# Turning two thirds of a gate and up product round: stationary weights in a routed expert kernel on one core

## The chip, the cores and the metric

The kernel runs on one core of one Trainium2 chip. The metric is the device time of one execution in microseconds. Before the change, three runs gave 753.37, 755.38 and 756.12 us; the median is 755.38.

A core has five engines with instruction streams of their own: TensorE (PE, whose weight loads are listed apart as PEld), VectorE (DVE), ScalarE (ACT), GpSimd (POOL) and SyncE (SP), which issues most transfers. They meet through semaphores. A matmul has a stationary operand, loaded by LDWEIGHTS, and a moving operand, whose columns are streamed through the array.

## The reference

One layer: layer norm, linear attention with a decaying state, a residual, a second layer norm, and a mixture of experts with one shared expert. The change touches the experts alone. With `x` of 4096 tokens by 256, 32 experts of 192 channels and 4 experts chosen for each token:

```python
g = jax.nn.silu(jnp.einsum('th,eih->tei', xf, gate_w))
u = jnp.einsum('th,eih->tei', xf, up_w)
routed = jnp.einsum('tei,ehi,te->th', g * u, down_w, combine)
sg = jax.nn.silu(xf @ shared_gate_w.T)
su = xf @ shared_up_w.T
shared = sg * su @ shared_down_w.T
return (routed + shared).reshape(b, s, h)
```

`combine` holds the softmax of the four best router scores times 1.8, and zero for the other experts. All is float32.

## The kernel before

The first part (`steps`, nine steps over eight sequences) does the attention and the router, and beside it loads, turns and splits expert weights. Each weight is kept in SBUF as two float16 halves, a high part and the rest, in one long tensor `W`: for each expert four blocks of gate and up (two halves of the 256 inputs, each high and low, each block GU = 384 columns wide: 192 gate and 192 up channels), and four blocks of down, 256 columns wide. Experts from the 24th on come from `w_late`, which the host lays out in that form (`laid_out`), and are split during the first tiles.

The second part is a loop over 191 tiles of 128 rows: 32 tiles of the shared expert, whose rows are tokens in order, then 159 routed tiles, each of one expert, whose rows were gathered into lists in DRAM. A tile goes through these stations:

- SP loads its rows (`load_tile`), already split into two float16 halves.
- PE turns them, `turn_in`, L1183: four transposes of 128x128 into PSUM. DVE copies the result to `xT` (`turn_out`, L1048) and signals `xT_done`.
- PE makes gate and up, L1212: six matmuls into `psG`, tokens stationary and the weights moving, 384 columns each (high by high, high by low, low by high, for each half of the inputs). The result has tokens on partitions and 384 channels along the free axis.
- ACT takes silu of the gate part (L664), DVE multiplies by the up part (L1072), ACT makes the high float16 half (L671, into `halves`), DVE the low one (L1091 and L1092) and signals `a_split`.
- PE turns this activation so that channels lie on partitions, L1232: three transposes of 128x128. The first 128 channels high, the remaining 64 high and low together, and the first 128 low. ACT copies them to `aT` (L668, 128x384) and signals `aT_done`.
- PE makes the down product, L1245: five matmuls of 256 columns with `aT` stationary. ACT scales it by the token's share (L680) and POOL adds it to an accumulator in DRAM by an indirect DMA (L640).

The order on each engine is written out by hand. `pe_tile(t)` issues in this order: the gate and up matmuls of tile t (behind the wait for `xT_done`), the register work of a routed tile, the turn of x for tile t+1 (L1183), the turn of the activation of tile t-1 (behind the wait for `a_split`), the down product of tile t-2 (behind `aT_done`), and more register work. The tiles overlap so that TensorE always has a stage of another tile to do.

The register work: a routed tile's weights lie at an offset in `W` that is known only at run time. `weights(t, off, width)` gives the slice, and `pe.lower_ap(...)` computes its address into registers ahead of its use, four for down at L1220 and four for gate and up of the next tile at L1249. Once in eight tiles the offsets of the next eight are fetched (`experts_of`, L1191 and L1193).

The last part of the kernel adds up three accumulators for each sequence and stores the output.

Of the kernel before, what the change touches and what calls it, by code (L numbers as in the profile page):

```python
# [5 lines left out]
def moe_block(nc, x, w_qkv, w_out, decay_param, router_w, router_b, gate_w, up_w, down_w,  # L6
# [6 lines left out]
    P = 128  # L13
# [35 lines left out]
    with ctx:  # L49
# [81 lines left out]
        half_word = carve(I)  # L131
        matched, share, token = carve(DEEP * K), carve(DEEP), carve(DEEP).bitcast(i32)
# [9 lines left out]
        halves = [words.bitcast(f16) for words in (half_word, carve(I))]  # L142
        aT = [carve(3 * P // 2).bitcast(f16).rearrange("p (n t) -> p n t", n=3) for _ in range(2)]
# [60 lines left out]
        psA = [bank[:, 0:3 * P // 2].bitcast(f16) for bank in (psV, psT[2])]  # L204
# [146 lines left out]
        def load_experts(eng, b):  # L351
# [3 lines left out]
            if b == 0:  # L355
                q0 = 1
                for src, dst in ((shared_gate_w[0:P], gu_nat[:, 0, 0]), (shared_gate_w[P:I], gu_nat[0:IC, 0, 1]),
                                 (shared_up_w[0:P - IC], gu_nat[IC:P, 0, 1]), (shared_up_w[P - IC:I], gu_nat[:, 0, 2]),
                                 (shared_down_w.rearrange("(c p) i -> p c i", p=P), dn_nat[:, 0, :, 0:I]),
                                 (shared_down_w[:, P:I].rearrange("(c p) i -> p c i", p=P), dn_nat[:, 0, :, I:I + IC])):  # L360
                    eng.dma_start(dst, src).then_inc(wstage_loaded, 16)
            e = PREP * b - 1 + q0
            which = slice(e, e + PREP - q0)
            for src, dst in ((gate_w[which, 0:P], gu_nat[:, q0:PREP, 0]), (gate_w[which, P:I], gu_nat[0:IC, q0:PREP, 1]),
                             (up_w[which, 0:P - IC], gu_nat[IC:P, q0:PREP, 1]), (up_w[which, P - IC:I], gu_nat[:, q0:PREP, 2])):
                eng.dma_start(dst, src.rearrange("e p h -> p e h")).then_inc(wstage_loaded, 16)
# [278 lines left out]
        def _(act):  # L645
# [11 lines left out]
            def act_tile(t):  # L657
# [7 lines left out]
                if a_tile(t - 1):  # L665
                    u = (t - 1) % 2
                    act.wait_ge(a_turned, t)
                    nc.scalar.activation(aT[u].rearrange("p n t -> p (n t)"), psA[u], ACT.Copy).then_inc(aT_done, 1)  # L668
                if a_tile(t):
                    act.wait_ge(a_done, t + 1)  # L670
                    nc.scalar.activation(halves[t % 2][:, 0:I], act32[t % 2], ACT.Copy).then_inc(a_hi_done, 1)  # L671
# [123 lines left out]
        def _(dve):  # L795
# [265 lines left out]
            def dve_tile(t):  # L1061
# [26 lines left out]
                if a_tile(t):  # L1088
                    dve.wait_ge(a_hi_done, t + 1)
                    both = halves[t % 2]  # L1090
# [21 lines left out]
        def _(pe):  # L1112
# [88 lines left out]
            def pe_tile(t):  # L1201
# [5 lines left out]
                if a_tile(t):  # L1207
                    pe.wait_ge(xT_done, t + 1)
                    n = 0
                    for sx, sw in ((0, 0), (0, 1), (1, 0)):  # L1210
                        for h in range(HC):
                            last = nc.tensor.matmul(psG[t % 2][:, 0:GU], xT[t % 2][:, sx, h], weights(t, (2 * h + sw) * GU, GU),  # L1212
                                                    start=(n == 0), stop=(n == 3 * HC - 1))
                            n += 1
# [13 lines left out]
                if a_tile(t - 1):  # L1228
                    u = (t - 1) % 2
                    pe.wait_ge(a_split, 2 * t)  # L1230
                    for n in range(3):
                        last = nc.tensor.transpose(psA[u][:, n * P:(n + 1) * P], halves[u][:, n * P:(n + 1) * P], ident16[:, :])  # L1232
                    last.then_inc(a_turned, 1)
# [6 lines left out]
                if a_tile(t - 2):  # L1240
                    u = t % 2
                    pe.wait_ge(aT_done, t - 1)
                    parts = ((0, 0, P), (1, 1, P), (2, 0, P), (0, 2, P), (1, 3, P))
                    for n, (part, q, height) in enumerate(parts):
                        last = nc.tensor.matmul(psY[u], aT[u][0:height, part], weights(t - 2, GUW + q * H, H, height), start=(n == 0), stop=(n == len(parts) - 1))  # L1245
                    last.then_inc(y_ready, 1)
                if routed_tile(t + 1):
                    for part in range(2 * HC):
                        pe.lower_ap(weights(t + 1, part * GU, GU))  # L1249
# [128 lines left out]
def laid_out(gate, up, down):  # L1378
# [4 lines left out]
    gu = _np.concatenate([gate, up], axis=1).reshape(n, 2 * i, h // 128, 128).transpose(0, 3, 2, 1).reshape(n, 128, -1)  # L1383
# [25 lines left out]
```

## Time and profile before

| | us |
|---|---|
| median of three runs | 755.38 |
| lowest and highest run | 753.37, 756.12 |
| span of the profiled execution, first to last instruction | 707.9 |
| between that span and the median of the runs | 47.5 |
| PE matmuls busy | 603.2 (85%) |
| DVE, ACT, POOL busy | 512.6, 434.9, 440.3 |
| mean granted clock of TensorE | 0.938 |

The profile records one execution. Its span runs from the first to the last instruction; what lies around it in a timed run isn't in it, and for the profiled execution only the span is on the page. So a change in the span is taken over to the median, with the 47.5 us left as they are. A busy time adds the stretches in which an engine has an instruction under way; matmuls are pipelined, so a record (say 220 ns for 128 columns) is longer than the distance from one to the next. That distance, not the record, is what a matmul costs in a full stream. Register work of TensorE's sequencer is not counted as busy but is listed when its line is asked for.

### The profile page before, as it was taken

What the parts mean: (1) busy time and instruction counts of PE and PEld (TensorE: products, weight loads), DVE (VectorE), ACT (ScalarE), POOL (GpSimd) and SP (SyncE); (2) the same over time, 40 slices, a digit from 0 to 9 for tenths busy, and PEclk for the clock granted to TensorE, in tenths of its full rate; (3) what the DMA queues carried; (4) which work ended last, traced back from release to release, by engine and by line L of the source; (5) the groups of instructions that cost most, each with busy time, mean ns of one, the idle gap of its engine ahead of it and who ended that gap; (6) DMA issues with size and microseconds to landing.
All of it is one profiled execution on the core that took longest, in us unless ns stands there. A gap on an engine that the chain in (4) does not pass through costs nothing.

```text
span 707.9 us, 15496 instructions
## 1 busy us (share of the span) xinstructions
PE 603.2 (85%) x4725; PEld 417.4 (59%) x4725; DVE 512.6 (72%) x1966; ACT 434.9 (61%) x1045; POOL 440.3 (62%) x367
## 2 busy tenths in 40 slices
PE   3898877897888899899999999999999999999000
PEld 2565544565555565677777777776777777776000
DVE  2588898989889968877766666666666666666164
ACT  2646445463636433688878878787788878788000
POOL 3031148658585776777078778887888888888300
PEclk9989999899999969999999999999999999999555
DMA  9664585959667676999589889888988888886799
GB/s 275 265 182 120 160 240 176 301 194 271 197 203 226 202 229 205 302 335 336 164 148 144 139 140 143 140 141 140 143 140 149 140 140 142 141 145 91 189 412 385
DMA packets 121460, 140.41 MB, mean 198 GB/s; under 512 B 22626, under 2 KB 110210, under 8 KB 120834
## 3 DMA queue, kind: packets, MB, share of 16 engines
q1 hardware_dynamic: 88816, 97.29, 44.4%
q0 software_dynamic: 29040, 38.68, 33.1%
q10 hardware_dynamic: 3522, 3.44, 1.5%
q8 instruction: 40, 0.66, 0.4%
q14 instruction: 42, 0.34, 0.2%
HBM read 79.19 MB, written 64.89 MB: 204 GB/s over the span
## 4 chain that ended last, share of the span: by engine, by line
PE 60%; DVE 19%; issue 6%; DMA 6%; POOL 4%; SPq 3%; ACT 2%; POOLq 0%; ACTq 0%; DVEq 0%
PE psD L1245 13%; PE psQ L1212 11%; PE psK L1212 11%; PE psT L1183 6%; PE psD L1296 4%; DMA acc_scratch<-arena 3%; DVE W L875 2%; DVE W L870 2%; SPq L514 2%; PE psK L1261 2%; PE psQ L1261 2%; DMA W<-acc_scratch 2%; PE psT L1232 2%; PE psV L1261 2%; PE psV L1232 2%
## 5 line engine op out<-in xcount | busy, mean ns | idle before, releaser
L640 POOL DMA_INDIRECT acc_scratch<-arena x159 | 251.3, 1581 | 73.2 <-issue 34.7
L586 POOL DMA_INDIRECT xlist_scratch<-list_row,dest x128 | 133.7, 1045 | 35.6 <-issue 34.1
L1245 PE MATMUL psD<-W,arena 128*128 (+1 forms) x955 | 135.5, 273 | 1.0 <-DVE arena L1044 0.9
L1048 DVE COPY arena<-psT 128x512 f16<-128x512 f16 x191 | 81.0, 424 | 69.2 <-PE psT L1183 68.6
L1212 PE MATMUL psK<-W,arena 128*128 (+1 forms) x576 | 109.3, 326 | 0.5 <-DVE arena L1048 0.5
L1212 PE MATMUL psQ<-W,arena 128*128 (+1 forms) x570 | 108.2, 326 | 0.1
L1245 PEld LDWEIGHTS psD<-W,arena 128*128 128x128 f16 x955 | 85.2, 98 | 8.0 <-DVE arena L1044 1.1
L671 ACT ACTIVATE arena<-arena 128x192 f16<-128x192 f32 x191 | 69.2, 362 | 13.9 <-DVE arena L1072 2.2
L680 ACT ACTIVATE arena<-psD,arena 128x256 f32<-128x256 f32 x159 | 72.8, 458 | 3.4 <-DMA acc_scratch<-arena 3.1
L1183 PE MATMUL psT<-ident,arena 128*128 128x128 f16 x764 | 74.0, 220 | 0.4 <-issue 0.4
L1183 PEld LDWEIGHTS psT<-ident,arena 128*128 128x128 f16 x764 | 57.0, 98 | 29.3 <-issue 7.2
L1091 DVE TENSOR_TENSOR arena<-arena 128x64 f16<-128x64 f32 x191 | 43.0, 225 | 40.4 <-ACT arena L671 40.4
L1212 PEld LDWEIGHTS psK<-W,arena 128*128 128x128 f16 x576 | 50.6, 97 | 33.7 <-DVE arena L1048 1.1
L1212 PEld LDWEIGHTS psQ<-W,arena 128*128 128x128 f16 x570 | 50.1, 97 | 32.4 <-DVE arena L1048 0.2
L566 POOL TENSOR_TENSOR W<-W 128x512 f32<-128x512 f32 x16 | 20.3, 1270 | 71.4 <-DVE W L870 71.3
L1092 DVE TENSOR_TENSOR arena<-arena 128x128 f16<-128x128 f32 x191 | 54.4, 285 | 0.0
L668 ACT ACTIVATE arena<-psT 128x384 f16<-128x384 f16 x95 | 46.6, 490 | 10.0 <-PE psT L1232 5.6
L668 ACT ACTIVATE arena<-psV 128x384 f16<-128x384 f16 x96 | 47.0, 490 | 7.4 <-PE psV L1232 2.1
L875 DVE SCALAR_TENSOR_TENSOR W<-psT,W 128x384 f16<-128x384 f32 (+1 forms) x72 | 40.0, 588 | 13.6 <-ACT W L720 13.6
L1296 PE MATMUL psD<-W 128*128 128x256 f32 x128 | 36.3, 447 | 11.6 <-DVE W L890 11.5
L720 ACT ACTIVATE W<-psT 128x384 f16<-128x384 f32 (+1 forms) x72 | 35.6, 528 | 16.5 <-PE psT L1139 8.5
L664 ACT ACTIVATE arena<-psK 128x192 f32<-128x192 f32 x96 | 31.7, 330 | 20.4 <-PE psK L1212 20.0
(164 smaller groups left out, 1084.8 us busy)
## 6 DMA issues: line engine op xcount, KB each, us to landing
arena<-xlist_scratch SPq DMA_DIRECT2D x159, 136.0 KB
W<-acc_scratch SPq DMA_DIRECT2D x24, 512.0 KB, 12.7
acc_scratch<-arena SPq DMA_DIRECT2D x16, 512.0 KB, 5.9
arena<-in_L_attn_x_dram SPq DMA_DIRECT2D x10, 512.0 KB, 5.1
arena<-in_L_ffn_down_w_dram SPq DMA_DIRECT2D x23, 192.0 KB, 4.9
xlist_scratch<-pad_scratch SPq DMA_DIRECT2D x32, 136.0 KB, 3.6
list_row<-xrow_scratch SPq DMA_DIRECT2D x32, 136.0 KB
acc_scratch<-arena SPq DMA_DIRECT2D x33, 128.0 KB, 12.4
```

The source lines that it names most:

```text
L586: nc.gpsimd.indirect_dma_start(xlist[:, :], bass.IndirectOffsetOnAxis(ap=dest[:, n:n + 1], axis=0), list_row[j % LISTS][:, :], None).then_ ...
L640: nc.gpsimd.indirect_dma_start(acc[t % ACCS][:, :], bass.IndirectOffsetOnAxis(ap=token[:, (t - NT) % DEEP:(t - NT) % DEEP + 1], axis=0), y ...
L668: nc.scalar.activation(aT[u].rearrange("p n t -> p (n t)"), psA[u], ACT.Copy).then_inc(aT_done, 1)
L671: nc.scalar.activation(halves[t % 2][:, 0:I], act32[t % 2], ACT.Copy).then_inc(a_hi_done, 1)
L680: nc.scalar.activation(y_sb[(t - 2) % ROUND], psY[t % 2], ACT.Copy, scale=share[:, (t - 2 - NT) % DEEP:(t - 2 - NT) % DEEP + 1]).then_inc( ...
L875: nc.vector.scalar_tensor_tensor(dst, bank_of("prep", n)[:, 0:width], WS, hi, ALU.mult, ALU.subtract).then_inc(prep_lo, 1)
L1048: nc.vector.tensor_copy(xT[t % 2].rearrange("p s c t -> p (s c t)"), psX[t % 2]).then_inc(xT_done, 1)
L1092: nc.vector.tensor_tensor(both[:, 2 * P:3 * P], act32[t % 2][:, 0:P], both[:, 0:P], ALU.subtract).then_inc(a_split, 1)
L1183: last = nc.tensor.transpose(psX[t % 2][:, n * P:(n + 1) * P], xg[t % XG][:, n * P:(n + 1) * P], ident16[:, :])
L1212: last = nc.tensor.matmul(psG[t % 2][:, 0:GU], xT[t % 2][:, sx, h], weights(t, (2 * h + sw) * GU, GU), start=(n == 0), stop=(n == 3 * HC - 1))
L1245: last = nc.tensor.matmul(psY[u], aT[u][0:height, part], weights(t - 2, GUW + q * H, H, height), start=(n == 0), stop=(n == len(parts) - 1))
L1296: last = nc.tensor.matmul(psD[:, j // 2, (j % 2) * H:(j % 2 + 1) * H], attnT[:, c, j * P:(j + 1) * P], wout_sb[:, c, :], start=(c == 0), s ...
```

## The change

Gate and up are made in three groups instead of one. The first 128 channels of gate, and the first 128 of up, are made with the weights stationary and the tokens moving, so they come out with channels on partitions, six matmuls of 128 columns for each. The remaining 64 of gate and 64 of up are made as before, together, in six matmuls of 128 columns, with tokens on partitions. For this the up weights are stored with their last 64 channels first, so that both remainders are adjacent. In `psG` each group lies where its channels lay, so that silu, product and split run unchanged.

The first 128 channels of the activation then already lie as the down product needs them, and their high and low halves are used straight from `halves`. Only the block with the 64 remaining channels (high and low) is turned and copied. `halves` gets a third buffer, since it is now read one tile later. The register work at the end of `pe_tile` prepares twelve slices instead of four: for each block two stationary operands (`for_matmul_weights=True`) and one moving one.

```diff
-        halves = [words.bitcast(f16) for words in (half_word, carve(I))]
-        aT = [carve(3 * P // 2).bitcast(f16).rearrange("p (n t) -> p n t", n=3) for _ in range(2)]
+        halves = [words.bitcast(f16) for words in (half_word, half_two, carve(I))]
+        aT = [carve(P // 2).bitcast(f16) for _ in range(2)]
...
-                    nc.scalar.activation(aT[u].rearrange("p n t -> p (n t)"), psA[u], ACT.Copy).then_inc(aT_done, 1)
+                    nc.scalar.activation(aT[u], psA[u], ACT.Copy).then_inc(aT_done, 1)
...
-                    n = 0
-                    for sx, sw in ((0, 0), (0, 1), (1, 0)):
-                        for h in range(HC):
-                            last = nc.tensor.matmul(psG[t % 2][:, 0:GU], xT[t % 2][:, sx, h], weights(t, (2 * h + sw) * GU, GU),
-                                                    start=(n == 0), stop=(n == 3 * HC - 1))
-                            n += 1
+                    products = [(sx, sw, h) for sx, sw in ((0, 0), (0, 1), (1, 0)) for h in range(HC)]
+                    whole = psG[t % 2][:, 0:GU]
+                    rest = whole.rearrange("p (m i) -> p m i", m=2)[:, :, P:I]
+                    for to, off in ((whole[:, 0:P], 0), (whole[:, I:I + P], 2 * P)):
+                        for n, (sx, sw, h) in enumerate(products):
+                            nc.tensor.matmul(to, weights(t, (2 * h + sw) * GU + off, P), xT[t % 2][:, sx, h],
+                                             start=(n == 0), stop=(n == len(products) - 1))
+                    for n, (sx, sw, h) in enumerate(products):
+                        last = nc.tensor.matmul(rest, xT[t % 2][:, sx, h], weights(t, (2 * h + sw) * GU + P, P),
+                                                start=(n == 0), stop=(n == len(products) - 1))
                     last.then_inc(gu_ready, 1)
...
                     pe.wait_ge(a_split, 2 * t)
-                    for n in range(3):
-                        last = nc.tensor.transpose(psA[u][:, n * P:(n + 1) * P], halves[u][:, n * P:(n + 1) * P], ident16[:, :])
-                    last.then_inc(a_turned, 1)
+                    nc.tensor.transpose(psA[u], halves[(t - 1) % 3][:, P:2 * P], ident16[:, :]).then_inc(a_turned, 1)
...
                     pe.wait_ge(aT_done, t - 1)
-                    parts = ((0, 0, P), (1, 1, P), (2, 0, P), (0, 2, P), (1, 3, P))
-                    for n, (part, q, height) in enumerate(parts):
-                        last = nc.tensor.matmul(psY[u], aT[u][0:height, part], weights(t - 2, GUW + q * H, H, height), start=(n == 0), stop=(n == len(parts) - 1))
+                    both = halves[(t - 2) % 3]
+                    high, rest, low = both[:, 0:P], aT[u], both[:, 2 * P:3 * P]
+                    parts = ((high, 0), (low, 0), (high, 2), (rest, 1), (rest, 3))
+                    for n, (part, q) in enumerate(parts):
+                        last = nc.tensor.matmul(psY[u], part, weights(t - 2, GUW + q * H, H), start=(n == 0), stop=(n == len(parts) - 1))
                     last.then_inc(y_ready, 1)
                 if routed_tile(t + 1):
                     for part in range(2 * HC):
-                        pe.lower_ap(weights(t + 1, part * GU, GU))
+                        for off in (0, 2 * P):
+                            pe.lower_ap(weights(t + 1, part * GU + off, P), for_matmul_weights=True)
+                        pe.lower_ap(weights(t + 1, part * GU + P, P))
...
-    gu = _np.concatenate([gate, up], axis=1).reshape(n, 2 * i, h // 128, 128).transpose(0, 3, 2, 1).reshape(n, 128, -1)
+    gu = _np.concatenate([gate, up[:, 128:], up[:, :128]], axis=1).reshape(n, 2 * i, h // 128, 128).transpose(0, 3, 2, 1).reshape(n, 128, -1)
```

Two more lines of `load_experts` load the up weights in the new order, with the same number and sizes of transfers, and `psA` shrinks like `aT`.

## Rows read from the trace of the kernel before

**Rows 1.** Part 1 of the page: busy us, share of the span, instructions.
```profile
PE 603.2 (85%) x4725; PEld 417.4 (59%) x4725; DVE 512.6 (72%) x1966; ACT 434.9 (61%) x1045; POOL 440.3 (62%) x367
```
**Rows 2.** By stretch: us; busy PE, PEld, DVE, ACT, POOL; clock; DMA share, GB/s.
```profile
280.20:345.00 64.80, 61.62 (x568) 44.49 (x569) 50.30 (x176) 51.85 (x142) 44.06 (x46) 1.00 0.90 296
345.00:655.50 310.50, 308.87 (x2879) 222.97 (x2878) 210.32 (x1118) 247.60 (x642) 245.61 (x156) 1.00 0.85 140
```
**Rows 3.** The chain that ended last, one routed tile: start us, us, what.
```profile
501.93 0.98 PE psK L1212 x6
502.91 0.22 PE psT L1183 x4
503.13 0.17 PE psT L1232 x3
503.30 0.55 PE psD L1245 x5
```
**Rows 4.** Timeline of a routed tile: start us, us, engine, line, operation, tiles, count.
```profile
352.03 1.14 PE L1212 MATMUL psQ<-W,arena 128*128 x6
...
352.77 0.28 DVE L1092 TENSOR_TENSOR arena<-arena 128x128 f16<-128x128 f32 x1
...
353.00 0.39 PE L1183 MATMUL psT<-ident,arena 128*128 128x128 f16 x4
...
353.39 0.71 PE L1245 MATMUL psD<-W,arena 128*128 x5
353.43 0.43 DVE L1048 COPY arena<-psT 128x512 f16<-128x512 f16 x1 [0.37 <-PE psT L1183]
...
353.90 0.78 PEld L1212 LDWEIGHTS psK<-W,arena 128*128 128x128 f16 x6
353.94 1.14 PE L1212 MATMUL psK<-W,arena 128*128 x6
...
354.68 0.29 DVE L1092 TENSOR_TENSOR arena<-arena 128x128 f16<-128x128 f32 x1
```
**Rows 5.** Timeline where the first tile's gate waits for the copy.
```profile
279.75 0.42 DVE L1048 COPY arena<-psT 128x512 f16<-128x512 f16 x1
...
280.22 0.50 PE L1212 MATMUL psK<-W,arena 128*128 128x384 f16 x2 [0.47 <-DVE arena L1048]
```
**Rows 6.** Line 1249 from 352 to 354: ns min/median/max, first to last start us.
```profile
L1249 PEldq FUSED_REGOPS  x2: 74/74/74, 353.1 to 353.3; - x2
```
**Rows 7.** A list-fetch tile from 353.8 to 355.5, by line; weight loads; waits, 300 to 650.
```profile
L1191 PEldq TENSOR_LOAD <-arena x1: 602/602/602, 353.9 to 353.9; - x1
...
L1193 PEldq FUSED_REGOPS  x1: 176/176/176, 354.6 to 354.6; - x1
...
L1220 PEldq FUSED_REGOPS  x2: 69/72/74, 354.8 to 354.9; - x2
...
355.06 0.23 PEld L1183 LDWEIGHTS psT<-ident,arena 128*128 128x128 f16 x4 [0.38 <-issue]
...
L1249 PEldq FUSED_REGOPS  x2: 74/76/79, 355.2 to 355.4; - x2
...
PEld psT L1183 <- issue: 7.2, 19, 0.6
```
**Rows 8.** Timeline of a router product, weight loads ahead of 32-column matmuls.
```profile
245.44 0.25 PEld L1348 LDWEIGHTS psD<-rwT,arena 128*128 128x128 f16 x6
```
**Rows 9.** Part 5 of the page: groups, busy us and mean ns of one.
```profile
L1183 PEld LDWEIGHTS psT<-ident,arena 128*128 128x128 f16 x764 | 57.0, 98 | 29.3 <-issue 7.2
...
L668 ACT ACTIVATE arena<-psT 128x384 f16<-128x384 f16 x95 | 46.6, 490 | 10.0 <-PE psT L1232 5.6
```
**Rows 10.** Line 1249 near 417.5, and the matmuls that stand ahead of it.
```profile
L1249 PEldq FUSED_REGOPS  x2: 74/74/74, 417.5 to 417.6; - x2
...
417.89 0.71 PE L1245 MATMUL psD<-W,arena 128*128 x5
```
**Rows 11.** Timeline of GpSimd in a routed tile.
```profile
500.93 1.56 POOL L640 DMA_INDIRECT acc_scratch<-arena  x1 [0.30 <-ACT arena L680]
```

More of the change, by code:

```diff
@@ L131, in moe_block @@
         half_word = carve(I)
+        half_two = carve(I)
         matched, share, token = carve(DEEP * K), carve(DEEP), carve(DEEP).bitcast(i32)
@@ L203, in moe_block @@
         psN = [psK, psQ]
-        psA = [bank[:, 0:3 * P // 2].bitcast(f16) for bank in (psV, psT[2])]
+        psA = [bank[:, 0:P // 2].bitcast(f16) for bank in (psV, psT[2])]
         psY = [psD[:, 0, 0:H], psD[:, 1, 0:H]]
@@ L357, in load_experts @@
                 for src, dst in ((shared_gate_w[0:P], gu_nat[:, 0, 0]), (shared_gate_w[P:I], gu_nat[0:IC, 0, 1]),
-                                 (shared_up_w[0:P - IC], gu_nat[IC:P, 0, 1]), (shared_up_w[P - IC:I], gu_nat[:, 0, 2]),
+                                 (shared_up_w[P:I], gu_nat[IC:P, 0, 1]), (shared_up_w[0:P], gu_nat[:, 0, 2]),
                                  (shared_down_w.rearrange("(c p) i -> p c i", p=P), dn_nat[:, 0, :, 0:I]),
@@ L364, in load_experts @@
             for src, dst in ((gate_w[which, 0:P], gu_nat[:, q0:PREP, 0]), (gate_w[which, P:I], gu_nat[0:IC, q0:PREP, 1]),
-                             (up_w[which, 0:P - IC], gu_nat[IC:P, q0:PREP, 1]), (up_w[which, P - IC:I], gu_nat[:, q0:PREP, 2])):
+                             (up_w[which, P:I], gu_nat[IC:P, q0:PREP, 1]), (up_w[which, 0:P], gu_nat[:, q0:PREP, 2])):
                 eng.dma_start(dst, src.rearrange("e p h -> p e h")).then_inc(wstage_loaded, 16)
@@ L667, in act_tile @@
                     act.wait_ge(a_turned, t)
-                    nc.scalar.activation(aT[u].rearrange("p n t -> p (n t)"), psA[u], ACT.Copy).then_inc(aT_done, 1)
+                    nc.scalar.activation(aT[u], psA[u], ACT.Copy).then_inc(aT_done, 1)
                 if a_tile(t):
                     act.wait_ge(a_done, t + 1)
-                    nc.scalar.activation(halves[t % 2][:, 0:I], act32[t % 2], ACT.Copy).then_inc(a_hi_done, 1)
+                    nc.scalar.activation(halves[t % 3][:, 0:I], act32[t % 2], ACT.Copy).then_inc(a_hi_done, 1)
                 if a_tile(t - 2):
@@ L1089, in dve_tile @@
                     dve.wait_ge(a_hi_done, t + 1)
-                    both = halves[t % 2]
+                    both = halves[t % 3]
                     nc.vector.tensor_tensor(both[:, I:2 * P], act32[t % 2][:, P:I], both[:, P:I], ALU.subtract).then_inc(a_split, 1)
```

## Prediction

> **What bounds the kernel now.** I read the page first, then the table by stretch, then the chain and one tile of the long middle stretch. The page gives 603 of 708 us of matmul time, and 61% to 72% for VectorE, ScalarE and GpSimd [rows 1]. The table shows where it lies: the tile loop runs from 280.2 to about 655 us, and in its second part (159 routed tiles) matmuls cover 308.9 of 310.5 us, with the clock granted in full (2.4 GHz) [rows 2]. The chain there holds nothing but TensorE: gate and up 0.98, turning x 0.22, turning the activation 0.17, down 0.55, so 1.91 us a tile [rows 3]. Matmul starts give the price of a matmul: 384 columns 0.975 / 6 = 162 ns, 256 columns 0.545 / 5 = 109 ns, and the seven of 128 columns from 353.00 to 353.39 take 55.7 ns each [rows 4]. So the engine is bound by columns, and not by loads or by waits, with two things close behind it.
>
> The first close thing is the turn of x. The last of the four L1183 matmuls starts at 353.17, the VectorE copy L1048 at 353.43, it takes 0.43, and the next gate matmul starts at 353.94 [rows 4]. Where that copy was really waited for, in tile 0, the gate started 0.05 us after its end (279.75 + 0.42 to 280.22) [rows 5]. So from the last L1183 start to the earliest possible gate it is 0.26 + 0.43 + 0.05 = 0.74 us; today it takes 0.77, which leaves 0.03.
>
> The second is TensorE's own sequencer. The prepared weight addresses (`lower_ap`) appear as FUSED_REGOPS of some 74 ns, two at L1249 and two at L1220 for each routed tile, so one for two addresses [rows 6, 7]. They hide as long as they are done before the wait for the copy ends. Once in eight tiles, where an address list is fetched (TENSOR_LOAD), they don't: the loads of x's turn start "<-issue" at 355.06, while the gate's six matmuls were through at 353.94 + 0.975 = 354.92: some 0.15 late [rows 4, 7]. From 300 to 650 us there are 19 such stalls [rows 7].
>
> **The change, part by part.** (1) Gate and up: six matmuls of 384 columns become 18 of 128. At 55.7 ns that is 1.003 for 0.975, +0.028 us a tile. Twelve more weight loads come with them. That a load hides behind 128 columns is seen in the seven at 55.7 ns, and more strongly at L1348, whose matmuls have 32 columns: six loads of 128x128 take 0.25 us together, which with 0.10 for the last is 0.03 from one to the next [rows 8]. I take 0 for the loads. The other reading is the length of a load's record, 98 ns [rows 9]; that bound stands in the rivals.
> (2) Two of three turns of the activation go: -2 x 0.056 = -0.111 us. The down product keeps five matmuls of 256 columns.
> (3) ScalarE's copy L668 shrinks from 384 to 128 columns. It takes 490 ns today [rows 9], so 0.16 if it went by columns alone, and at most 0.49 if the length did not matter. Either way it is off the path, since PE waits for nothing in the routed tiles [rows 2]. Worth nothing. A third `halves` buffer and the new order of `up` rows change no count or size: 0.
> (4) TensorE alone would so need 1.003 + 0.223 + 0.056 + 0.545 = 1.827, 0.083 less than 1.91. But the shortened part lies between the turn of x and the next gate. There now stand 0.056 + 0.056 + 0.545 = 0.66 us from the last L1183 start, and the copy needs 0.74. The wait for xT_done takes the place of the two turns, and the tile becomes 1.003 + 0.167 + 0.74 = 1.91. So nothing is gained, in shared tiles as well. Queued behind that wait are the whole gate product and the next turn of x, on which VectorE waits.
> (5) Addresses: L1249 prepares 12 instead of 4, six FUSED_REGOPS instead of two. They stand behind the wait for a_split and ahead of the wait for xT_done. Their pace comes from the list-fetch tile: from the gate's first load at 353.90 to 355.06 is 1.16, the four instructions sum to 0.602 + 0.176 + 0.074 + 0.069 = 0.92, which leaves 0.05 to 0.06 for each step between; so one takes 0.13 to 0.14 from start to start [rows 4, 7]. The path in two tiles: the gate starts at 352.03 and its L1092 ends at 354.97, 2.94 later, 2.97 with the 0.028 of (1). Then about 0.07 to the first address op (L1092's end at 353.05, the op at "353.1") [rows 4, 6], five steps of 0.135, 0.074 for the last and 0.06 to the gate: 2.97 + 0.07 + 0.81 = 3.85 for two tiles, 1.925 a tile. That is later than the copy (1.91), so the address ops become the last to arrive: +0.0135 x 159 = +2.1 us. Bounds: 1.91 (pace 0.13 or less, where the copy is last again, +0) and 1.95 (pace 0.145, +6).
> (6) List-fetch tiles (20). Behind a released wait the sequencer runs through the gate's 12 instructions almost at once (TENSOR_LOAD at 353.9, first load 353.90). After this change the sequencer comes late itself, and then it takes about 6 ns an instruction: 24 of them between the load at 355.06 and the address op at 355.2 [rows 7]. The gate is now 36 instructions, so TENSOR_LOAD starts about 0.2 after the gate. Then 1.10 as before and 0.05 to the turn of x, 1.35; to its last matmul 0.17, copy and gate 0.74: 2.26, by the address ops (20 instructions 0.11, then 0.81) about the same. The excess over a plain tile is 0.33, today 0.15: +0.18 x 20 = +3.7 us. Bounds: 0 (instructions as fast as behind a released wait; +0.05 x 20 = +1) and 0.4 late (+8).
> That needs the 36 to fit in the queue; if only some 20 do, TENSOR_LOAD waits for 16 of them, 8 matmuls or 0.4 us, which is the upper bound. The trace shows at least 16 waiting: the address op of L1249 at 417.5 comes, in program order, behind the three turns and five down products of its tile, each a load and a matmul, and the down products begin at 417.89 only [rows 10]. The Trainium skill (TensorE: Matmul & The Clock Gate, the table at its head) says the queue holds 64; by that the 36 fit, and no row here shows more than the 16 to 20 of this one.
> (7) Slack elsewhere. In the shared tiles matmuls cover 61.6 of 64.8 us [rows 2], so 3.2 us are waits. The shorter L668 and the fewer turns may give back 0 to 1 of them; I take -0.5.
> Sum: +2.1 + 3.7 - 0.5 = **+5.3 us**. The profiled span of 707.9 becomes 713.2; the 47.5 us between it and the median of the runs (755.4) is taken over: **760.7 us**.
>
> **Rivals.** A: the address ops keep ahead (a faster pace, or fewer ops) and the list fetch is no later. The tile is bound by the copy at 1.91, and the sum is -0.5 to +1.5: about 756. For it: the difference of 1.925 and 1.91 is smaller than what a tenth of a microsecond in the rows can fix. Against: at the list fetch the ops are seen in the way. B, the gain comes through: TensorE runs at 1.83 to 1.86. It would need the copy to start earlier than 0.26 after the turn. GpSimd needs 1.56 and 0.30 of issue for each routed tile, 1.86 [rows 11], so the most would be 0.05 x 159 + 0.08 x 25 = 10 us, 745. I see nothing that moves the copy. C, the addresses cost more: a stationary operand takes more than half a FUSED_REGOPS, so eight to twelve ops; two more are 0.27 in two tiles, +21 us, 782; it decides from the seventh op on. D, weight loads don't hide behind 128 columns: 12 x 0.098 + 6 x 0.056 = 1.51 for the gate, +0.51 x 191 = +97 us, 852; rows 8 speak against it.
> The Trainium skill (same page, Back-to-back issue gap) has a sustained rate of some 81 ns for each pair of load and 128-column matmul. By that the gate would be 1.46 and the total near 840, and rows 4 and 8, at 56 and 30 ns, contradict it.
>
> **How the numbers follow.** Forecast (both address effects) 0.64, A 0.20, B 0.03, C 0.09, D 0.04. The range takes in A and the upper bounds of (5) and (6): 755 to 770; below it lie B and a little of A, above it C and D. A difference of about 0.5% (3.8 us) is what a measurement can tell from none. Faster than that only in B: 0.03. Within: A and a fifth of the forecast, where both effects are near their low ends: 0.20 + 0.13, 0.33. Slower: the rest, 0.64.
>
> **What would show it.** In the after trace: L1183's last start to the next gate stays 0.74 or more, though only one turn lies between, and TensorE idles about 0.1 us ahead of the gate; L1249 has six address ops a tile, and a plain routed tile takes 1.91 (A) or 1.925; shared tiles take 1.91; list-fetch tiles some 2.26 instead of 2.06; matmuls of the new gate start 56 ns apart. It would be wrong if a tile falls below 1.90, if the 18 matmuls take over 1.05 us, or if L1249 shows more than six ops.

## The result and the profile after

Four runs of the kernel after gave 758.03 to 769.46 us, median 762.23; the kernel before, beside it, 755.13 (753.37 to 756.12). The ratio is 1.0141, with a 95% interval of 1.0082 to 1.0200: slower, by 6 to 15 us. The two medians differ by 7.1 us (0.9%), at the low end of that interval. The forecast was 760.7, which is +5.3.

The profiled execution of after is the longest of the four, 769.46 us; its span is 767.7. That is 60 us more than the profiled span of before (707.9), and most of it is no work of the change. A second chip, on which before takes about 705 us, shows the two kernels side by side without it: there after took 715.14 us (six runs), ratio 1.0123, interval 1.0079 to 1.0168. I therefore read both: after, and **a_again**, the same kernel on the second chip (span 714.7).

Part 1 of the page, after and then a_again (busy us, share, instructions); compare [rows 1]:

```profile
PE 618.1 (81%) x6635; PEld 480.8 (63%) x6635; DVE 513.3 (67%) x1966; ACT 386.4 (50%) x1045; POOL 435.9 (57%) x367
```
```profile
PE 607.9 (85%) x6635; PEld 474.3 (66%) x6635; DVE 513.1 (72%) x1966; ACT 387.6 (54%) x1045; POOL 440.1 (62%) x367
```

By stretch, columns as in [rows 2], shared tiles and then routed tiles (first gate of the one to first gate of the other, then to the gate of the last tile): after, a_again, and **b_again**, the kernel before on the second chip.

```profile
284.66:394.77 110.11, 72.64 (x903) 62.77 (x904) 51.41 (x180) 46.19 (x145) 41.06 (x43) 0.81 0.56 177
394.77:712.70 317.93, 311.04 (x4424) 267.35 (x4424) 207.75 (x1107) 202.11 (x632) 240.03 (x155) 1.00 0.77 134
```
```profile
277.61:344.71 67.10, 62.78 (x904) 55.00 (x903) 51.27 (x182) 45.83 (x147) 43.29 (x44) 1.00 0.87 285
344.71:659.70 314.99, 310.93 (x4424) 267.36 (x4425) 207.72 (x1103) 203.41 (x632) 239.83 (x155) 1.00 0.80 137
```
```profile
276.86:342.11 65.25, 62.56 (x581) 45.31 (x582) 51.25 (x179) 53.13 (x145) 42.93 (x45) 1.00 0.90 299
342.11:648.90 306.79, 305.04 (x2845) 220.16 (x2845) 208.03 (x1107) 244.63 (x633) 240.21 (x154) 1.00 0.85 140
```

On one chip the routed part grew from 306.8 to 315.0 us, the shared part from 65.3 to 67.1. ScalarE has 41 us less to do in the routed part, and nobody gains by it. The 110 us of shared tiles in after are taken up further down.

The chain of a routed tile in a_again, which answers to [rows 3] (start, us, what):

```profile
564.00 0.76 PE psK L1215 x12
564.76 0.34 PE psK L1218 x6
565.10 0.22 PE psT L1184 x4
565.32 0.06 PE psT L1236
565.38 0.55 PE psD L1250 x5
```

L1215 are the twelve weights-stationary matmuls, L1218 the six others, L1184 the turn of x, L1236 the turn of the activation, L1250 down. The twelve take 0.76 here where 12 x 55.7 ns is 0.67: the rest is a wait. The timeline of that tile names it, as [rows 4] did before:

```profile
563.92 0.67 PEld L1215 LDWEIGHTS psK<-arena,W 128*128 x12 [0.20 <-DVE arena L1049]
...
564.69 0.28 DVE L1093 TENSOR_TENSOR arena<-arena 128x128 f16<-128x128 f32 x1
...
564.93 0.39 PE L1184 MATMUL psT<-ident,arena 128*128 128x128 f16 x4
...
565.21 0.71 PE L1250 MATMUL psD<-W,arena 128*128 x5
565.13 0.33 ACT L665 ACTIVATE arena<-psK 128x192 f32<-128x192 f32 x1 [0.25 <-PE psK L1218]
...
565.36 0.42 DVE L1049 COPY arena<-psT 128x512 f16<-128x512 f16 x1 [0.38 <-PE psT L1184]
...
565.70 0.35 DVE L1073 SCALAR_TENSOR_TENSOR arena<-psK,arena 128x192 f32<-128x192 f32 x1
...
565.84 0.45 PEld L1215 LDWEIGHTS psQ<-arena,W 128*128 x8 [0.20 <-DVE arena L1049]
```

From the last start of L1184 (564.93 + 3 x 0.056 = 565.10) to the next gate is 0.74 us, as forecast, and the gate's loads follow the copy (565.36 + 0.42) by 0.06.

The same copy delays a second path. VectorE's product (L1073) could follow the silu, which ends at 565.46, but the copy stands ahead of it on VectorE, and it starts at 565.70. Behind the product come the split and, on TensorE's sequencer, the address ops. So some 0.2 us of the address ops' own path is this copy; in the kernel before the product waits in the same way.

The waits of the routed part sum it up (engine line waited for: us, times, longest); first a_again, then the kernel before:

```profile
PEld psK L1215 <- DVE arena L1049: 19.5, 79, 0.4
PEld psQ L1215 <- DVE arena L1049: 16.8, 79, 0.3
PEld psT L1184 <- issue: 6.0, 19, 0.5
```
```profile
PEld psT L1183 <- issue: 6.9, 18, 0.6
PEld psV L1232 <- DVE arena L1092: 0.6, 1, 0.6
```

In each of the 158 tiles the loads of the gate wait for the copy of x (0.23 us on average). The matmuls lose less, 0.76 - 0.67 = 0.09 us in the tile above, since in a full stream the loads run ahead of them. In before no such row exists.

**Tile by tile** (distances between the first gate matmuls of neighbouring tiles): a plain tile is 1.912 us in before. In after most are 1.917 to 1.922, and some (27 of 139 in a_again) 1.924 to 1.935, where an address op comes last. But after has late tiles. In each eight, one list-fetch tile of 2.1 to 2.5 (mean of 19: 2.24 in a_again, 2.29 in after; 2.08 in before, and 2.16 in b_again), and two to three more, mostly 1.98 to 2.08 (55 of the 139 tiles without a fetch in a_again are above 1.935, 54 in after); b_again has none of these. The address ops show why. Some of the six in a plain tile, and then some in a late one (571.75 begins the next gate); duration, first to last start:

```profile
L1255 PEldq FUSED_REGOPS  x4: 74/74/74, 565.0 to 565.7; - x4
...
L1255 PEldq FUSED_REGOPS  x3: 74/74/74, 570.8 to 571.2; - x3
...
L1256 PEldq FUSED_REGOPS  x1: 74/74/74, 571.5 to 571.5; - x1
...
571.75 0.34 PEld L1215 LDWEIGHTS psK<-arena,W 128*128 x6 [0.26 <-DVE arena L1049]
```

Six ops, 0.133 us apart. In 70 of 152 routed tiles of a_again (from the fifth on) one step of the six is longer, 0.17 to 0.29 (571.214 to 571.499 here), and since the ops and the copy arrive together in a plain tile (the last op's end is 0.056 ahead of the gate, the copy's 0.06), such a step moves the gate. The view names the copy, which had long been done; the op came last.

### The profile page after: what moved, and what is told of

It reads as the page before. It is cut to its first block, busy times and chain, and to the rows that moved or that the text cites. A ratio compares the mean times of both kernels' runs of the same rounds, so it can differ in the third digit from the quotient of the medians.

```text
span 767.7 us, 19952 instructions
## 1 busy us (share of the span) xinstructions
PE 618.1 (81%) x6635; PEld 480.8 (63%) x6635; DVE 513.3 (67%) x1966; ACT 386.4 (50%) x1045; POOL 435.9 (57%) x367
## 4 chain that ended last, share of the span: by engine, by line
PE 62%; DVE 14%; issue 8%; another core or an unknown queue 3%; DMA 3%; POOL 3%; ACT 3%; SPq 2%; POOLq 0%; ACTq 0%; DVEq 0%
PE psD L1250 13%; PE psQ L1215 10%; PE psK L1215 10%; PE psT L1184 6%; PE psQ L1218 4%; PE psK L1218 4%; PE psD L1303 3%; SPq L515 2%; PE psQ L1268 2%; PE psK L1268 2%; DMA W<-acc_scratch 2%; DVE W L876 2%; DVE W L871 2%; PE psV L1268 2%
## 5 line engine op out<-in xcount | busy, mean ns | idle before, releaser
L641 POOL DMA_INDIRECT acc_scratch<-arena x159 | 247.7, 1558 | 105.6 <-issue 43.6
L1250 PE MATMUL psD<-W,arena 128*128 (+1 forms) x955 | 136.5, 274 | 1.2 <-DVE arena L1045 1.1
L1215 PE MATMUL psQ<-arena,W 128*128 128x128 f16 x1140 | 82.5, 224 | 25.6 <-DVE arena L1049 14.9
L1215 PEld LDWEIGHTS psQ<-arena,W 128*128 (+1 forms) x1140 | 66.3, 100 | 46.4 <-DVE arena L1049 28.4
L1250 PEld LDWEIGHTS psD<-W,arena 128*128 128x128 f16 x955 | 86.0, 99 | 8.7 <-DVE arena L1045 1.5
L1215 PE MATMUL psK<-arena,W 128*128 128x128 f16 x1152 | 82.4, 222 | 8.7 <-issue 5.4
L1215 PEld LDWEIGHTS psK<-arena,W 128*128 (+1 forms) x1152 | 66.2, 99 | 30.8 <-DVE arena L1049 21.1
L1184 PE MATMUL psT<-ident,arena 128*128 128x128 f16 x764 | 75.4, 222 | 3.6 <-issue 2.9
L1184 PEld LDWEIGHTS psT<-ident,arena 128*128 128x128 f16 x764 | 51.0, 99 | 7.0 <-issue 6.8
L1218 PE MATMUL psQ<-W,arena 128*128 (+1 forms) x570 | 48.7, 223 | 0.0
L1218 PE MATMUL psK<-W,arena 128*128 (+1 forms) x576 | 48.2, 220 | 0.0
L665 ACT ACTIVATE arena<-psQ 128x192 f32<-128x192 f32 x95 | 31.4, 331 | 30.9 <-PE psQ L1218 26.0
```

The source lines that it names most:

```text
L641: nc.gpsimd.indirect_dma_start(acc[t % ACCS][:, :], bass.IndirectOffsetOnAxis(ap=token[:, (t - NT) % DEEP:(t - NT) % DEEP + 1], axis=0), y ...
L665: nc.scalar.activation(gate, psG[t % 2][:, 0:I], ACT.Silu, scale=1 / WS).then_inc(silu_done, 1)
L1184: last = nc.tensor.transpose(psX[t % 2][:, n * P:(n + 1) * P], xg[t % XG][:, n * P:(n + 1) * P], ident16[:, :])
L1215: nc.tensor.matmul(to, weights(t, (2 * h + sw) * GU + off, P), xT[t % 2][:, sx, h], start=(n == 0), stop=(n == len(products) - 1))
L1218: last = nc.tensor.matmul(rest, xT[t % 2][:, sx, h], weights(t, (2 * h + sw) * GU + P, P), start=(n == 0), stop=(n == len(products) - 1))
L1250: last = nc.tensor.matmul(psY[u], part, weights(t - 2, GUW + q * H, H), start=(n == 0), stop=(n == len(parts) - 1))
```

## The experiments

All ratios are against the kernel before on the same chip. First the two kernels as they are, on one chip.

**a_again, b_again: both kernels unchanged.**

> The kernel before, unchanged, profiled once more. The profile of before has a span of 707.9 us though its runs take 755, and the profile of the changed kernel has 45 us of waits in the shared tiles, with one of 19 us in tile 0, that the profile of before does not have. Theory: those waits belong to both kernels, the first profile of before was an execution without them, and this one has a span near 753 us, shared tiles (first to 33rd gate) of about 110 us instead of 66, and routed tiles of 1.912 us as before. Rival: the waits are the change's own; then the span here is again near 708 and the shared tiles take 66 us.

> The changed kernel, unchanged, in five rounds, for the size of the difference. Expected 1.007 to 1.012 times before (760 to 764 us); plain routed tiles 1.92 us, list-fetch tiles 2.26 to 2.29, and in each eight tiles two more that are 0.06 to 0.1 late.

Measured: 704.55 (ten runs), ratio 0.9992 (0.9957 to 1.0028), and 715.14, ratio 1.0123. The expectation on the long shared part failed: neither kernel has it here. The mechanism in the routed tiles is that of after; the list-fetch tiles are slightly shorter than expected (2.24) and the other late ones more than two in eight.

**a_static, b_static: no address work.** In both kernels the routed tiles read fixed weights, the calls of `lower_ap` and the list fetch go.

```diff
-                return W[0:height, bass.ds(at_of[t] + (EW + off), width)]
+                return W[0:height, EW + off:EW + off + width]
```

> The changed kernel with fixed weight addresses: every routed tile uses the weights of one expert, so the routed part of the result is another one, and neither the address operations nor the list fetches are on TensorE's sequencer. Theory (the loss is the sequencer's address work, above all in list-fetch tiles): all routed tiles 1.92 us, bound by the copy of x, no late ones, routed part 15.4 us for eight tiles instead of 15.9, so 8 to 10 us less than the changed kernel: about 753. Rival (the 18 short matmuls with their weight loads cost the time): at most 2 us less, about 761.

> The kernel before with fixed weight addresses, in the same way. The address work is hidden in before except for the list fetches, 0.15 us in 20 tiles and some 0.3 in three of them: 3 to 4 us less than before, 751 to 752, all plain tiles 1.912. The changed kernel with fixed addresses should then be only 191 x 0.01 = 2 us above this one; if the 18 short matmuls are the loss it is 7 above.

Measured: a_static 705.81, ratio 0.9991 (0.9958 to 1.0024), b_static 701.1, ratio 0.994 (0.9898 to 0.9981). So by the medians address work costs after 9.3 us (715.14 - 705.81) and before 3.5 (704.55 - 701.1). A plain tile of a_static stays at 1.921, and the late tiles are gone but for 7 of 139:

```profile
340.72:646.20 305.48, 304.13 (x4426) 267.95 (x4423) 208.48 (x1105) 204.77 (x632) 238.92 (x154) 1.00 0.83 142
```

305.5 us against 315.0 in a_again. Without addresses the tile is bound by the copy alone, and it is still not shorter than before's 1.912: the two turns saved bring nothing. Between the two static kernels lie 4.7 us, 2.8 of them in the routed part, where I had expected 2, or 7 if the short matmuls were the loss. Of the 2.8, 158 x 0.009 = 1.4 is the plain tile; the rest are single late tiles, and the remaining 2 us are within what the medians can tell.

**a_turns: two idle turns put back.**

```diff
                     pe.wait_ge(a_split, 2 * t)
+                    for n in range(2):
+                        nc.tensor.transpose(psI[u][:, n * P:(n + 1) * P], halves[(t - 1) % 3][:, 2 * n * P:(2 * n + 1) * P], ident16[:, :])
```

> The kernel after, with two more 128x128 transposes between the wait for a_split and the real turn of the activation; their results are read by nobody. So the three turns of the kernel before are back, while gate and up are made the new way. Theory (the gain of 0.111 us from two turns less is eaten by the wait for the copy): of the 0.111 put back, 0.08 to 0.1 fills TensorE's idle time ahead of the gate; a plain tile goes from 1.920 to at most 1.95, the whole to 0 to 5 us above the kernel after. Rival (turns are on the path, and it was 18 matmuls and their loads that took their gain): 0.111 x 191 = 21 us above the kernel after, 2.03 a tile.

Measured: 713.57 (nine runs), ratio 1.0096 (1.0061 to 1.0131), no more than after itself. A plain tile is 1.942 instead of 1.921, and the waits for the copy are down from 36.3 us to 1.4 (0.8 for psQ and 0.6 for psK):

```profile
PEld psQ L1216 <- DVE arena L1050: 0.8, 4, 0.2
```

The 0.111 us put back cost 0.021; 0.09 fell into the wait. What they add to a plain tile they give back in late ones: there are seven beside the list fetches, where a_again has 55, and the routed part is 314.4 us for 315.0. That is not the extra slack alone: only 12 of 152 tiles have a long step among their six address ops, where a_again has 70. Why the long steps fall outside the row here isn't shown.

**a_early: the copy out of the way.** The turn of x for the next tile goes ahead of the last six gate matmuls, so that 0.99 us of matmuls lie behind it.

```diff
+                    if a_tile(t + 1):
+                        turn_in(t + 1)
                     for n, (sx, sw, h) in enumerate(products):
                         last = nc.tensor.matmul(rest, xT[t % 2][:, sx, h], weights(t, (2 * h + sw) * GU + P, P),
...
-                if a_tile(t + 1):
-                    turn_in(t + 1)
```

> The kernel after, with the turn of x for the next tile moved ahead of the last six gate and up matmuls (twelve weights-stationary ones, the four turns of x, six with tokens stationary, the turn of the activation, down). Now 0.06 + 0.335 + 0.056 + 0.545 = 0.99 us of matmuls lie between the last turn of x and the next gate, more than the 0.74 that the copy needs. Theory (copy and address ops arrive together, 1.92 a tile): taking the copy away alone gains next to nothing, since the six address ops still come behind the wait for a_split; a plain routed tile stays at 1.91 to 1.93, the shared tiles, which have no address ops, fall to about 1.84, and the whole is 2 to 3 us below the kernel after, some 6 to 8 above before. Rival (only the copy binds, the address ops have slack): 1.84 in routed tiles too, 0.08 x 191 = 15 us below the kernel after and 5 below before. Second rival (gate's end 0.22 later delays the chain silu, product, split, address ops): 2.0 or more a tile, slower than after by over 10 us.

Measured: 712.17 (11 runs), ratio 1.0105 (1.0073 to 1.0136). The wait for the copy is gone, and its place is taken:

```profile
PEld psQ L1215 <- issue: 24.4, 77, 0.4
PEld psK L1215 <- issue: 6.6, 32, 0.5
```

"issue" is the sequencer. The last address op of such a tile and the gate's loads behind it:

```profile
L1255 PEldq FUSED_REGOPS  x1: 74/74/74, 520.3 to 520.3; - x1
...
520.38 0.67 PEld L1215 LDWEIGHTS psQ<-arena,W 128*128 x12 [0.30 <-issue]
```

The address ops alone hold the gate now. Most shared tiles are 1.83 or 1.92, routed tiles alternate, often between 1.838 and 2.03 to 2.09 (mean 1.942 without the list fetches, so the expected 1.91 to 1.93 failed), and the routed part is 314.8 us. Taking the copy off the gate's path gained 0.2 us there.

The edit doesn't take away the copy and nothing else. It ends the gate 0.22 us later, and silu, product, split and address ops hang on that end, as the second rival says. Most of it comes back, because the product no longer stands behind the copy:

```profile
517.96 0.33 ACT L665 ACTIVATE arena<-psQ 128x192 f32<-128x192 f32 x1 [0.62 <-PE psQ L1220]
...
518.32 0.36 DVE L1073 SCALAR_TENSOR_TENSOR arena<-psQ,arena 128x192 f32<-128x192 f32 x1 [0.28 <-ACT arena L665]
```

The product follows the silu by 0.03 us, where a_again has 0.23, and the split ends 3.01 us after the gate's start instead of 2.98. So the address ops arrive even slightly later than in a_again: 1.838 + 2.035 = 3.87 us for two tiles, where it has 3.84. Whether they would still hold the gate if the copy itself were faster, without a later end of the gate, is not tested.

**a_split: half of the address ops out of the way.** Six of twelve addresses are prepared right behind the turn of x, ahead of the wait for `a_split` (in list-fetch tiles all stay behind it).

```diff
+            def ahead(t):
+                return 0 if (t + 4 - NT) % BATCH == 0 else 2
...
+                prepare(t, 0, ahead(t))
                 if a_tile(t - 1):
...
+                prepare(t, ahead(t), 2 * HC)
```

> The kernel after, with the first six of the twelve addresses prepared right behind the turn of x, ahead of the wait for a_split (except in list-fetch tiles, where all twelve stay behind it). Three address ops instead of six then stand between the end of the split and the next gate, 0.4 us less. Theory: a plain tile stays at 1.92, because the copy binds (0.74 from the last turn of x to the gate), but the tiles of 1.985 and 2.017 us, where one address op comes 0.09 to 0.15 late, go back to 1.92; up to 8 us of the 9.4 that they and the list fetch cost are in reach, I expect 2 to 6 below the kernel after. Rival (address ops alone bind): the tile falls below 1.90. Rival (the late tiles come from something else than the address ops behind the wait, such as the fetch of instructions as such): nothing changes, late tiles stay.

Measured: 711.74 (12 runs), ratio 1.0085 (1.0055 to 1.0116). Beside the list fetches nearly all routed tiles are 1.920 or 1.921 (one is above 1.935, at 1.954); the routed part is 310.7 us, 4.3 less than a_again, although the list-fetch tiles, at a mean of 2.30 for 2.24, lost 1.2. So the late tiles, and those of about 1.93, come from address ops behind that wait: the same ops earlier, and they are gone. The copy is still waited for, with either bank of PSUM alike:

```profile
PEld psQ L1225 <- DVE arena L1049: 15.5, 79, 0.2
```

**a_both: both edits.**

> Both edits together: the turn of x ahead of the last six gate and up matmuls, and half of the addresses ahead of the wait for a_split. Theory: with the copy and the address ops both out of the way TensorE itself binds, 1.015 + 0.223 + 0.056 + 0.545 = 1.84 us a tile (or GpSimd with 1.86); plain routed tiles 1.84 to 1.87, list-fetch tiles about 2.3, total 10 to 16 us below the kernel after and 0 to 7 below before: the two edits together give more than the sum of each alone. Rival (something else, such as the chain from the gate's end over silu, product and split, holds a tile at 1.92): total as the better one of the two single edits.

Measured: 707.26 (12 runs), ratio 1.0028 (0.9997 to 1.0060). A plain tile falls to 1.838, TensorE's own 1.83:

```profile
512.31 0.67 PE psQ L1225 x12
512.98 0.22 PE psT L1184 x4
513.20 0.34 PE psQ L1230 x6
513.53 0.06 PE psV L1247
513.59 0.55 PE psD L1261 x5
```

The routed part is 304.4 us: 10.6 below a_again, where the single edits gave 0.2 and 4.3. Each of these is from one profile. By the medians the whole is 7.9 us below a_again, where the single edits gave 3.0 and 3.4, so there the surplus isn't clear of the noise; the plain tiles, 1.838 for 1.92, decide it. Both expected totals were missed, the 10 to 16 us below after and the 0 to 7 below before: the whole is 2.0 us above before, with an interval that reaches 1. Against b_again 139 plain tiles gain 0.074 us each, 10 us. The list fetch takes half of it back: a tile with one has a mean of 2.45, where I had expected about 2.3 and b_again has 2.16, (2.45 - 2.16) x 19 = 5.5 us, and a few single late tiles take 2.4. That leaves the routed part 2.4 us below b_again's; where the other 4 us between the medians lie, one profile each doesn't show.

**a_fetch, b_fetch: the list for 16 tiles at a time**, with the op that follows the fetch one tile later, in a_both and in before.

```diff
+            FETCH = 2 * BATCH
...
-                pe.load(expert_at[batch % 2], owner_i[0:1, BATCH * batch:BATCH * (batch + 1)])
+                pe.load(expert_at[batch % 2], owner_i[0:1, FETCH * batch:FETCH * (batch + 1)])
```

> The kernel a_both (turn of x ahead of the last six gate matmuls, half of the addresses ahead of the wait for a_split), with the list of experts fetched for 16 tiles at a time instead of eight, and the register op that follows the fetch moved into the next tile. Theory (what is left in a_both above 1.84 us a tile is the fetch on TensorE's sequencer, 0.3 to 0.75 us in each of 20 tiles): ten such tiles fewer, 4 to 7 us below a_both, that is 2 to 5 us below the kernel before. Rival (fetch time grows with the number of words): no change.

> The kernel before with the same edit of the fetch alone (16 tiles at a time, the register op one tile later). Ten tiles with a fetch cost 0.15 to 0.45 us less: 2 to 4 us below the kernel before. It tells how much of a_fetch's gain belongs to the change under study, and how much could be had without it.

**a_words: the list for two tiles at a time**, in a_both, with half of the addresses always early.

> The kernel a_both, with the list of experts fetched for two tiles at a time in every second tile, instead of for eight, and half of the addresses always ahead of the wait for a_split. The fetch of 8 words took 0.59 us or more and that of 16 words 1.10 or more, so it goes by the words, some 0.064 each, and 2 words should take 0.2 at most. In a_both's plain tiles TensorE's sequencer stands idle for about 0.37 us ahead of the wait for a_split and 0.15 ahead of the wait for the copy. Theory (a small fetch fits in that idle time, a large one doesn't): routed tiles of 1.83 to 1.88 throughout, no list-fetch tile above 1.95, 20 x 0.5 = 8 to 12 us below a_both in the routed part, which is 6 to 10 us below the kernel before. Rival (each fetch has a fixed cost of some 0.5 us, or its register op and steps add up to more than the idle time): every second tile 2.0 or more, 10 us or more above a_both.

Measured (b_fetch, a_fetch and b_18 on a chip where before takes 750.6, a_words on one where it takes 706.7): b_fetch 750.62, ratio 1.0000 (0.9974 to 1.0026); a_fetch 756.81, ratio 1.0077 (1.0048 to 1.0107); a_words 720.48, ratio 1.0202 (1.0157 to 1.0246). What I expected of them failed in all three; a_words did what its rival says (every second tile above 2.0, some 12 us above a_both by the ratios). The fetch itself, min/median/max in ns, for 8 words (a_again), 16 (b_fetch) and 2 (a_words):

```profile
L1192 PEldq TENSOR_LOAD <-arena x19: 590/658/867, 352.6 to 640.0; - x19
```
```profile
L1192 PEldq TENSOR_LOAD <-arena x10: 1107/1321/1516, 375.4 to 656.6; - x10
```
```profile
L1193 PEldq TENSOR_LOAD <-arena x77: 532/537/837, 345.1 to 655.1; - x77
```

Two words cost nearly what eight do, 16 cost twice as much. I had put a line through 8 and 16 and read 0.064 us a word; the shortest fetches are 0.53 for two, 0.59 for eight and 1.11 for 16. In a_words every second routed tile is mostly 2.20 to 2.27, the others 1.830, and the routed part 322 us. Two at a time is worse than eight. 16 at a time gained nothing in before (ratio 1.0000), and a_fetch, on another chip, has no better ratio than a_both.

**b_18: the finer matmuls alone.** The kernel before, with 18 matmuls of 128 columns, tokens stationary throughout, three turns.

```diff
+                    for off in (0, P, 2 * P):
+                        for n, (sx, sw, h) in enumerate(products):
+                            last = nc.tensor.matmul(psG[t % 2][:, off:off + P], xT[t % 2][:, sx, h], weights(t, (2 * h + sw) * GU + off, P),
```

> The kernel before, with gate and up made in 18 matmuls of 128 columns instead of six of 384, all with tokens stationary; the three turns of the activation stay. It has the finer matmuls of the change (and its twelve addresses, six address ops), without its gain of two turns. Theory (18 matmuls cost 0.03 to 0.04 us more than six, weight loads cost nothing, and TensorE's stream binds at 1.912 + 0.03 to 0.04): a plain tile of 1.94 to 1.95, the whole 6 to 10 us above the kernel before; the address ops (1.925) stay just inside the tile. Rival (short matmuls with a load each cost more, 81 ns each or the 98 ns of a load's record): gate 1.46 to 1.5, a tile of 2.4, the whole about 90 us above before.

Measured: 766.09 (six runs), ratio 1.0195 (1.0149 to 1.0242), 15.4 us above before. The gate of one tile in its chain:

```profile
542.37 1.01 PE psQ L1212 x18
```

A plain tile is 1.942, +0.030, so matmuls and loads cost what was forecast, and no 81 ns each. The total is 5 us more than the upper end of my expectation. List-fetch tiles have a mean of 2.29, and 30 of the other 139 are late as in after (by their mean, 1.970 for 1.942, worth 4 us); the shared part on this chip adds to it, below.

## Why the prediction was right, and where it was off

**Right by the working.** Step (1): the 18 matmuls start 55.7 ns apart and the weight loads hide; the last starts 0.96 after the first. The gate takes 1.015 rather than 1.003, because its first load is issued only when the wait ends and the second matmul follows by 0.066. Rival D and the rule of the Trainium skill (TensorE: Matmul & The Clock Gate, Back-to-back issue gap) of 81 ns a pair fall; b_18 and the chain of a_both, TensorE at 1.83 a tile, say the same. Step (4): the wait for the copy takes the place of the turns, 0.74 to the digit; a_static shows the copy alone holding a tile at 1.921, a_turns that 0.09 of the two turns fits into the wait, and a_both that the tile falls to TensorE's own once copy and address ops are both out of the way. Step (5): six address ops in every tile, at a pace of 0.133. Rival C (seven or more) falls.

**Right in direction, off in size.** (5) forecast 1.925 a plain tile, with the address ops last; it is mostly 1.920 to 1.921, the same as in a_static, where there are no ops, so the copy is last there and the ops are 0.01 us or less behind it or ahead: +0.009 x 139 = 1.3 us. (Rival A said 1.91 for want of the 0.012 that the gate takes longer.) What (5) missed is that a row of ops isn't even: its long steps, 0.04 to 0.15 us over the pace, make two to three more late tiles in each eight. The 139 routed tiles without a fetch have a mean of 1.960 in a_again and 1.912 in b_again, 6.7 us in all, so the long steps are worth 5.4, the largest single part; a_split took them away. The ops stood in my sum with a mean pace and no spread, though I had put their arrival within 0.015 of the limit. (6) forecast 0.18 a fetch; the fetch starts 0.07 to 0.13 behind the gate's first matmul and not 0.2 (so it didn't wait until 8 of the 18 were through, and the queue held the gate), its tile came to 2.24 and 2.29 as forecast (2.26), and the change of it was 0.08 in a_again against b_again and 0.21 in after against before (1.5 to 4 us): the fetch's own time varies from 0.59 to 0.95 from one to the next, and I had one row of it. (7) gave back 0.5; the shared part grew by 1 to 2 us instead, of which 32 x 0.009 is the tile.

Measured on one chip, in one profile each: 8.2 us in the routed part (1.3 + 5.4 + 1.5) and 1.8 in the shared, 10 in all, where +5.3 was forecast; the medians there differ by 9.4. On the first chip the medians differ by 7.1, within an interval of +6.2 to +15 that +5.3 just misses. So 762.2 for 760.7 is closer than the sum deserves. There is luck in one more number: (5) and (6) put +5.8 us on the address work, and the static kernels give 9.3 - 3.5 = 5.8, but it comes mostly from the long steps, which the prediction doesn't have, and not from the fetch or a later plain tile.

**Wrong: the 47.5 us "around the span".** I took the difference between the span (707.9) and the median (755.4) as something outside the program. It isn't: on every run whose span and time belong together they differ by 1.7 to 1.9 us. The profile of before then belongs to an execution of about 710 us and the three times to others of 755. What differs most is the shared part. On one set of chips before takes 705 us and its shared tiles 65 to 66; on the others 750 to 755 and, in b_fetch, before but for its fetch, 98.6:

```profile
284.94:383.52 98.58, 69.80 (x582) 47.79 (x583) 51.55 (x179) 52.18 (x144) 37.75 (x39) 0.86 0.60 187
```

The same stretch in after is 110 us, with 0.81 of the clock (1.00 on the second chip). Of the 43 us more than in a_again, 19 are lost at once, in the first tile, the rest in shorter waits up to the 20th; the timeline of after in the first tile:

```profile
301.62 0.96 POOL L587 DMA_INDIRECT xlist_scratch<-list_row,dest  x1 [0.30 <-issue]
304.62 0.33 ACT L665 ACTIVATE arena<-psK 128x192 f32<-128x192 f32 x1 [19.34 <-remote]
305.35 0.33 SPq L412 DMA_DIRECT2D arena<-xrow_scratch  x1
305.36 0.42 DVE L1049 COPY arena<-psT 128x512 f16<-128x512 f16 x1 [19.32 <-remote]
```

ScalarE and VectorE stand still for 19 us, SyncE's queue for 16 and TensorE for 14, while GpSimd issues one indirect store after the other; 2 to 3 us after the end of the last of them all go on. That the stores are what they wait for is argued from this order; the profile names no releaser it knows ("remote"). A late delivery of instructions would look alike and isn't excluded: in the shared tiles of after TensorE's gate matmuls wait 16 us more on "issue", in pieces of up to 5.9, where b_fetch has 9 and a_again none. VectorE's wait in the first tile is 15 us in b_fetch. So it is in both kernels, so it is no work of the change. Whether the change makes it longer stays open: the profiles with 18 matmuls a gate have 110, 113 and 111 us there (after, b_18, a_fetch), the one with six has 98.6, while on the second chip all kernels have 65 to 67. That would be the part of b_18 and a_fetch that the routed tiles don't explain (a_fetch is 1.7 us below b_fetch in the routed part and 6.2 above it in all). One profile each doesn't settle it: b_fetch's is of the shortest of its 12 executions (747.97), those of after and b_18 of their longest (769.46 and 769.6), and only a_fetch's (756.81) is of a middle one. And no run takes the indirect stores away.

## What to carry to other kernels

Taking work off the engine that is bound helps only as far as the next arrival, and there may be two at the same instant: here the copy of x and the address ops. Moving either out of the way gave 0.2 or 4.3 us in the routed part, moving both 10.6; test such causes one at a time and together. And look whether the two hang together: here the copy also stands ahead of the product on VectorE, which the address ops wait for, so moving it changes the other path too. Splitting a matmul with a run-time address multiplies register work on TensorE's sequencer: count it as a row of instructions behind the last wait, with its late ones, and move it ahead of the wait. And before a difference between a span and a time is called overhead, look for an execution of which both are known.

## What the runs showed of the chip that I had not expected

Two chips differ by 45 us on the kernel before (750.6 and 705.8), and in the profiles 33 us (b_fetch and b_again) to 43 us (after and a_again) lie in one stretch of 32 tiles.
